# Decoder kernel: the experts' low-rank output in two float32r passes instead of one float32 product

## The chip, the cores and the metric

The kernel runs on one core of a Trainium2 chip. The core has TensorE (PE, matrix products, with a second queue PEld for loading weights), VectorE (DVE), ScalarE (ACT), GpSimd (POOL) and SyncE (SP, which issues most DMAs). Time is device microseconds of the core for one execution; a run takes the kernel before beside a changed one on the same chip.

## The reference, cut to what matters

Two decoder layers over T = 1024 rows of D = 512. The part at hand is the feed-forward of layer 0: a dense product, plus a low-rank output whose rank (8, 16, 32 or 64) is chosen for each row by the largest of four gate scores.

```python
RANKS = (8, 16, 32, 64)
out = jnp.einsum('bsd,od->bso', hidden_states, W) + b
x = hidden_states.reshape(-1, d_in)
scores = x @ gate_w.T + gate_b
...
lora_outputs = jnp.stack([x @ A[:r, :].T @ B[:, :r].T for r in RANKS], axis=1)
sel = jnp.take_along_axis(lora_outputs, selected[:, :, None], axis=1)
...
x = _layernorm(x + _L0_ffn_ref(x, ...), axis=-1)
```

With one expert chosen its weight is 1, so the kernel computes x·Aᵀ (64 columns), sets the columns over the chosen rank to zero, and multiplies by B once. All is float32.

## The kernel before

All engines run programs written out by hand, in order, with semaphores between them. Rows are cut into NT = 8 blocks b of 128. The steps of the feed-forward of layer 0, by engine (line numbers are those of the profile):

- PE `ranks(b)` (L872): x·[Aᵀ, gate columns], 112 columns, into half of a PSUM bank. `ffn_W(b)` (L882): the dense product, four float32 products of 512 columns, into one of three banks (FF_BANK); block b takes the bank of block b-3, so from b = 3 on it waits (L880) for the addition that empties it, `plus` of block b-3. `lora_T(b)` (L886): transposes the masked 64 columns. `lora_out(b)` (L890): adds one float32 product of 65 rows (64 ranks and a row of ones for the bias b) to the bank of `ffn_W(b)`.
- DVE `choose(b)` (L1960 to L1965): four short linked instructions, gate scores, two maxima, mask, and the masked copy `lm`. `ln_head(16+b)`: `plus` (L1804) reads the bank, adds the residual into `rbuf`; then the row statistics (L1788, L1789). `x_low` (L1810): the low part of the normalised, transposed rows.
- ACT `lora_T_out(b)` (L1450): copies the transposed 64 x 128 part into `lmT`. `norm_tail` (L1281) normalises, `x_T_out` (L1274) copies transposed blocks.
- POOL: the reciprocal root of each block's variance.

Between these stand pieces of other work: `early_bends` on ACT (L1224 to L1240) and `unit_part` on DVE (L1739, L1745, L1757) unpack the 4-bit weights of layer 1; `attention_lora`/`add_lora` (L901, L1974) and `attention_product`/`m_low_of` (L912, L1998) fold that layer's attention weights into one matrix; `stack_low_of`, `down_stack_low` (L1980, L1982, L1987) make low parts of small matrices.

The loop over t = 0 to 7 has, on PE, in this order: `lora_T(t)`, two products of `attention_lora` (t up to 3), `ffn_W(t+2)`, `ranks(t+2)`, `lora_out(t)`, and from t = 2 on `x_T(2, t-2)`; from t = 3 on `attention_product` stands among them. `ffn_W(3)`, of t = 1, is the first that waits for a `plus`. On DVE: from t = 3 `x_low`, two `add_lora` (t up to 3), a piece of a low part, unpacking, `choose(t+2)`, `m_low_of`, `ln_head(16+t)`, unpacking. Before the loop DVE does `choose(0)`, `turn_norm(15)`, `choose(1)`; ACT's last step before the loop is `x_T_out(15)`.

A float32r product takes operands rounded to float32r. Elsewhere the kernel already replaces a float32 product by three such passes: high·high, high·low and low·high (L1030 to L1032).

Of the kernel before, what the change touches and what calls it, by code (L numbers as in the profile page):

```python
# [135 lines left out]
def decoder_kernel(nc, i, out):  # L136
# [4 lines left out]
    with ctx:  # L141
        def sb(name, shape, dt=F32):
            return ctx.enter_context(nc.sbuf_tensor(name, shape, dt))
# [24 lines left out]
        with nc.sbuf_tensor("a_down", [STACK, FF], F32) as a_down:  # L168
            pass
        ad_st = sb("ad_st", [STACK, FF], F32R)  # L170
        folded_m = sb("folded", [P, T])
        ff_s = sb("ff_s", [P, SLOTS, 2])
        with nc.sbuf_tensor("arena_r", [P, NF * T], F32R) as arena_r:
# [12 lines left out]
        minus_half = sb("minus_half", [P, 1])  # L186
        small = sb("small", [P, 2, 32])
        gate_v = sb("gate_v", [P, 2, NL + 3 * SEG])
        lmT = sb("lmT", [P, 2, P])
        probT = lmT  # L190
        prob = sb("prob", [P, 2, P])
        threes = prob[:, 0, :]
        qk_b = sb("qk_b", [P, 1])
# [11 lines left out]
        def carve(memory, start, n):  # L205
            return memory[:, start:start + n], start + n
# [21 lines left out]
        qkT, w_at = carve(early_w, w_at, KD * 2 * HA)  # L228
        wv, w_at = carve(early_w, w_at, KD * HA)
        s_qkv, w_at = carve(early_w, w_at, 3 * KD * NB)  # L230
        lm, w_at = carve(early_w, w_at, 2 * RMAX)
        assert w_at <= 2 * CH
        qkT, wv, lm = qkT.rearrange("p (j c) -> p j c", j=KD), wv.rearrange("p (j c) -> p j c", j=KD), lm.rearrange("p (s c) -> p s c", s=2)
        wsum, woT, shared, xT, agT = (m.rearrange("p (j c) -> p j c", j=KD) for m in (wsum, woT, shared, xT, agT))
        w0T = wq1 = shared
        wk1 = [m[:, 0:D] for m in (bT0, bT_d, wk2, wk3)]
        lora_l = wo0
        ad_high = wh[:, :, :].rearrange("p s c -> p (s c)")[:, 0:FF]
        m_lo = [arena_r[:, m_at:m_at + D] for m_at in (wk3_at, free_at, free_at + D, wo0_at)]

# [201 lines left out]
        def _(sp):  # L442
# [159 lines left out]
        def _(pe):  # L602
# [259 lines left out]
            def ranks(b):  # L862
                pe.wait_ge(xt_ready, NT + b + 1)
                if b == 0:
                    pe.wait_ge(in_ffn0, 48)
                    pe.wait_ge(kq_ready, NT - 1)
                elif b == 1:
                    pe.wait_ge(kq_ready, NT)
                if b >= 2:
                    pe.wait_ge(lmT_ready, b - 1)  # L870
                for k in range(KD):
                    last = pe.matmul(turn_bank(b)[:, 0:RMAX + NL], xT[:, k, b * P:(b + 1) * P], agT[:, k, :],  # L872
                                     start=(k == 0), stop=(k == KD - 1))
                last.then_inc(ag_ps, 1)
# [8 lines left out]

            def lora_T(b):
                pe.wait_ge(lm_ready, b + 1)
                pe.transpose(turn_bank(b)[0:RMAX, P:2 * P], lm[:, b % 2, :], ident[:, :]).then_inc(lm_ps, 1)  # L886

            def lora_out(b):
                pe.wait_ge(lmT_ready, b + 1)
                pe.matmul(bank[FF_BANK[b % 3]][:, :], lmT[0:RMAX + 1, b % 2, :], bT0[0:RMAX + 1, :], start=False, stop=True).then_inc(f0_ps, 1)  # L890

            def attention_lora(n):

# [324 lines left out]
        def _(act):  # L1218
# [226 lines left out]
            def lora_T_out(b):  # L1445

                act.wait_ge(lm_ps, b + 1)
                if b >= 2:
                    act.wait_ge(f0_ps, b - 1)
                nc.scalar.activation(lmT[0:RMAX, b % 2, :], turn_bank(b)[0:RMAX, P:2 * P], ACT.Copy).then_inc(lmT_ready, 1)  # L1450

            for t in range(NT):
                lora_T_out(t)
# [270 lines left out]
        def _(dve):  # L1724
# [93 lines left out]
            link(nc.vector.tensor_reduce(k_one[:, 0:1], ident[:, :].rearrange("p (i r) -> p r i", r=ROWG)[:, HD, :], AX.X, ALU.add))  # L1818
            nc.vector.tensor_scalar(k_one[:, 1:2], k_one[:, 0:1], -1.0, None, ALU.mult).then_inc(blanked, 1)
            nc.vector.memset(ones8[:, :, :], 0.0)  # L1820
            nc.vector.memset(lmT[RMAX:RMAX + 1, :, :], 1.0)
            nc.vector.memset(wb[:, 2 * KD:2 * KD + 1], 0.0)
            nc.vector.memset(ones[:, :], 1.0)
            link(nc.vector.memset(picked[:, :], 0.0))
# [128 lines left out]
            def choose(b):  # L1953
                s = b % 2
                ps = turn_bank(b)
                logits, sides, mask = (gate_v[:, s, n:n + size] for n, size in ((0, NL), (NL, 2 * SEG), (NL + 2 * SEG, SEG)))
                dve.wait_ge(ag_ps, b + 1)
                if b == 0:
                    dve.wait_ge(in_bias, 16 * 3)
                link(nc.vector.tensor_tensor(logits, ps[:, RMAX:RMAX + NL], g_b[:, :], ALU.add))  # L1960
                link(nc.vector.tensor_reduce(sides, logits.rearrange("p (n r) -> p n r", r=3), AX.X, ALU.max))
                link(nc.vector.tensor_tensor(mask, sides[:, 0:SEG], sides[:, SEG:2 * SEG], ALU.is_gt))
                if b >= 2:
                    dve.wait_ge(lm_ps, b - 1)
                nc.vector.tensor_tensor(lm[:, s, :].rearrange("p (r m) -> p r m", m=SEG), ps[:, 0:RMAX].rearrange("p (r m) -> p r m", m=SEG),  # L1965
                                        mask.unsqueeze(1).to_broadcast([P, RMAX // SEG, SEG]), ALU.mult).then_inc(lm_ready, 1)

            def add_lora(n):

# [5 lines left out]

            def stack_low_of(part):

                dve.wait_ge(stack_hi, part + 1)
                if part == 0:
                    nc.vector.tensor_tensor(a_st[2 * RG:STACK, :], a_gu[2 * RG:STACK, :], f32(a_st[2 * RG:STACK, :]), ALU.subtract).then_inc(stack_low, 1)  # L1980
                else:
                    nc.vector.tensor_tensor(bd_st[RG:2 * RG, :], bT_d[RG:2 * RG, :], f32(bd_st[RG:2 * RG, :]), ALU.subtract).then_inc(stack_low, 1)  # L1982

            def down_stack_low():

                dve.wait_ge(stack_hi, 4)
                nc.vector.tensor_tensor(ad_st[2 * RG:STACK, :], a_down[2 * RG:STACK, :], f32(ad_high[2 * RG:STACK, :]), ALU.subtract).then_inc(stack_low, 1)  # L1987

            def b_lower(j):

                dve.wait_ge(stack_hi, 4 + j + 1)
                part = b_st[RG:2 * RG, j % 2, :]
                nc.vector.tensor_tensor(part, b_gu[RG:2 * RG, j % 2, :], f32(part), ALU.subtract).then_inc(stack_low, 1)

# [259 lines left out]
def layout(a):  # L2254
# [42 lines left out]
    def pairs(m):  # L2297
# [4 lines left out]
        "qkT": rows(c(qkv[:2 * HA].T)), "wv": rows(c(qkv[2 * HA:].T)), "qk_b": c(f["L0_attn_Wqk_b"].reshape(HA, 2).T.reshape(P, 1)),  # L2302
        "v_b": c(np.concatenate([f["L0_attn_Wv_b"]] * 2)[:, None]), "wo0": wo0,
        "w0T": rows(c(f["L0_ffn_W"].T)), "agT": rows(np.concatenate([f["L0_ffn_A"][rank_at].T, np.stack([gate_w[n] for n in LOGITS], 1)], 1)),
        "bT0": np.concatenate([f["L0_ffn_B"].T[rank_at], f["L0_ffn_b"][None]]), "g_b": np.array([[gate_b[n] for n in LOGITS]], np.float32),
        "c_qkv": pairs(ca[:3].reshape(3 * KD, P, D)), "c_o": pairs(ca[3].T.reshape(KD, P, D)),
        "s_qkv": c(sa[:3].reshape(3, KD, P, NB).transpose(2, 0, 1, 3).reshape(P, -1)),
        "s_o": pairs(sa[3].T.reshape(KD, 2, D)), "lora_l": lora_l, "lora_r": lora_r,
# [25 lines left out]
```

## Time and profile before

| | us |
|---|---|
| median of 3 runs | 645.32 (645.03 to 645.48) |
| the profiled execution | 645.23 |
| its span, first to last instruction | 643.1 |
| PE busy | 632.0 |
| DVE busy | 396.3 |
| ACT busy | 381.6 |

The span is what the trace covers; 2.1 us of the profiled execution lie around it. "Busy" of PE counts from the start of a product to its modelled end, and products overlap, so the distance from one start to the next tells more than the duration. A float32 product appears as two records, a float32r product and a transpose as one.

### The profile page before, as it was taken

The page shows a single profiled execution, that of the slowest core. Times are in us where ns is not written, and L with a number is a line of the kernel's source. Part 1 is how long each engine was busy: PE and PEld are TensorE (multiplying, and loading weights), DVE is VectorE, ACT ScalarE, POOL GpSimd, SP SyncE. Part 2 cuts the span into 40 slices and gives each one's busy share as a digit, 9 for nine tenths or more (in the row PEclk, how much of TensorE's full clock was granted, in tenths as well). Part 3 has the DMA queues.
Part 4 walks back from the last instruction along what each step waited for, and adds up shares of the span by engine and source line. Part 5 has one row for each costly group of instructions (what it writes and reads, how often), then busy time and mean ns, then how long its engine had stood idle before and what let it go on. Part 6 is the DMA issues. An engine that isn't in the chain of part 4 may idle for free.

```text
span 643.1 us, 8521 instructions
## 1 busy us (share of the span) xinstructions
PE 632.0 (98%) x3226; PEld 470.0 (73%) x3226; DVE 396.3 (62%) x633; ACT 381.6 (59%) x527; POOL 65.0 (10%) x116
## 2 busy tenths in 40 slices
PE   9999999999999999999999999999999999999996
PEld 6655555544558888888888888887777888888874
DVE  4798787667988777767667355335655212125467
ACT  2977789976987697576675154223565343316532
POOL 1032142311330000000000000001211000000012
PEclk9999999999999999999999999999999999999999
DMA  7771585512253134233320003056010322100002
GB/s 246 288 243 52 188 268 172 162 52 92 81 152 120 39 110 139 73 104 111 94 83 2 1 1 131 1 216 274 1 33 2 115 77 88 33 1 0 1 33 99
DMA packets 25590, 63.92 MB, mean 99 GB/s; under 512 B 5541, under 2 KB 10725, under 8 KB 24782
## 3 DMA queue, kind: packets, MB, share of 16 engines
q1 hardware_dynamic: 23294, 61.68, 29.4%
q10 hardware_dynamic: 2256, 1.70, 0.8%
q8 instruction: 26, 0.43, 0.3%
q14 instruction: 14, 0.11, 0.1%
HBM read 58.77 MB, written 4.60 MB: 99 GB/s over the span
## 4 chain that ended last, share of the span: by engine, by line
PE 88%; DVE 4%; ACT 4%; DMA 1%; issue 1%; SPq 1%; POOL 0%; POOLq 0%; DVEq 0%; ACTq 0%
PE bank L1043 18%; PE bank L1031 8%; PE bank L1030 8%; PE bank L1032 8%; PE bank L1122 8%; PE bank L1121 8%; PE bank L882 4%; PE bank L802 3%; PE bank L606 3%; PE bank L741 2%; PE bank L1097 1%; DMA codes<-in_c_qkv 1%; PE bank L912 1%; PE bank L926 1%; PE bank L984 1%
## 5 line engine op out<-in xcount | busy, mean ns | idle before, releaser
L1232 ACT ACTIVATE line<-line 128x1024 f32<-128x1024 f32 x87 | 91.4, 1050 | 0.2
L1030 PE MATMUL bank<-xh,wh 128*128 128x512 f32 x224 | 87.5, 391 | 0.0
L1031 PE MATMUL bank<-xl,wh 128*128 128x512 f32 x224 | 87.5, 391 | 0.0
L1032 PE MATMUL bank<-xh,wl 128*128 128x512 f32 x224 | 87.3, 390 | 0.0
L1043 PE MATMUL bank<-wh,xh 128*128 128x512 f32 x192 | 76.1, 396 | 0.2 <-DVE xl L2128 0.2
L1043 PE MATMUL bank<-wh,xl 128*128 128x512 f32 x192 | 74.9, 390 | 0.0
L2211 DVE SCALAR_TENSOR_TENSOR arena<-bank,ff_s,arena 128x512 f32<-128x512 f32 x28 | 21.0, 752 | 72.9 <-PE bank L1122 63.8
L2128 DVE TENSOR_TENSOR xl<-arena,xh 128x1024 fp32r<-128x1024 f32 (+1 forms) x26 | 29.7, 1141 | 35.4 <-ACT xh L1536 35.3
L1121 PE MATMUL bank<-xh,wh 128*128 128x512 f32 x128 | 50.3, 393 | 0.0
L1536 ACT ACTIVATE xh<-arena 128x1024 fp32r<-128x1024 f32 (+1 forms) x26 | 25.6, 991 | 41.3 <-PE bank L1043 34.8
L1122 PE MATMUL bank<-xl,wh 128*128 128x512 f32 x128 | 49.9, 390 | 0.0
L1032 PEld LDWEIGHTS bank<-xh,wl 128*128 128x128 f32 x224 | 42.1, 188 | 8.8
L1030 PEld LDWEIGHTS bank<-xh,wh 128*128 128x128 f32 x224 | 42.1, 188 | 8.5
L1031 PEld LDWEIGHTS bank<-xl,wh 128*128 128x128 f32 x224 | 42.1, 188 | 8.5
L1630 ACT ACTIVATE arena<-bank,ff_s 128x512 f32<-128x512 f32 x28 | 19.2, 686 | 43.4 <-PE bank L1122 43.4
L1512 ACT ACTIVATE arena<-bank 128x512 f32<-128x512 f32 x28 | 16.4, 586 | 46.9 <-PE bank L1032 46.9
L1695 POOL TENSOR_TENSOR rstd<-rstd,minus_half 128x1 f32<-128x1 f32 x40 | 26.7, 668 | 172.1 <-DVE rstd L2149 162.4
L1043 PEld LDWEIGHTS bank<-wh,xh 128*128 128x128 f32 x192 | 36.1, 188 | 8.3 <-DVE xl L2128 0.6
L1043 PEld LDWEIGHTS bank<-wh,xl 128*128 128x128 f32 x192 | 36.1, 188 | 7.5
L1121 PE MATMUL bank<-xh,wl 128*128 128x512 f32 x96 | 37.6, 391 | 0.0
L1745 DVE SCALAR_TENSOR_TENSOR line<-line 128x1024 f32<-128x1024 f32 x29 | 35.3, 1218 | 3.6 <-ACT line L1232 3.2
L1043 PE MATMUL bank<-wl,xh 128*128 128x512 f32 x96 | 37.4, 390 | 0.0
(219 smaller groups left out, 1264.3 us busy)
## 6 DMA issues: line engine op xcount, KB each, us to landing
codes<-in_c_gu SPq DMA_DIRECT2D x14, 512.0 KB, 3.8
scales<-in_s_gu SPq DMA_DIRECT2D x28, 256.0 KB, 4.0
codes<-in_t_gu SPq DMA_DIRECT2D x8, 512.0 KB, 4.2
codes<-in_c_dn SPq DMA_DIRECT2D x7, 512.0 KB, 4.6
scales<-in_s_dn SPq DMA_DIRECT2D x14, 256.0 KB, 3.9
fold<-in_t_dn SPq DMA_DIRECT2D x1, 3584.0 KB, 15.7
codes<-in_c_qkv SPq DMA_DIRECT2D x6, 512.0 KB, 4.8
scales<-in_t_gu SPq DMA_DIRECT2D x6, 512.0 KB, 3.8
```

Of the source, the lines that this page charges most:

```text
L882: pe.matmul(bank[FF_BANK[b % 3]][:, :], xT[:, k, b * P:(b + 1) * P], w0T[:, k, :], start=(k == 0), stop=False)
L1030: pe.matmul(dst, wh[:, s, c:c + P], xh[:, k, cols], start=(k == 0), stop=False)
L1031: pe.matmul(dst, wh[:, s, c:c + P], xl[:, k, cols], start=False, stop=False)
L1032: last = pe.matmul(dst, wl[:, s, c:c + P], xh[:, k, cols], start=False, stop=(k == KD - 1))
L1043: ins = pe.matmul(dst, h[:, b * P:(b + 1) * P], w, start=first and p == 0, stop=last and p == len(hiddens) - 1)
L1121: pe.matmul(dst, w[:, c:c + P], xh[:, k, cols], start=(k == 0), stop=False)
L1122: last = pe.matmul(dst, w[:, c:c + P], xl[:, k, cols], start=False, stop=(k == KD - 1))
L1232: nc.scalar.activation(below(slot), below(slot), ACT.Prelu, bias=bias, scale=scale, alpha=alpha).then_inc(bent, 1)
L1536: nc.scalar.activation(dst[:, cols], hT[:, j, cols], ACT.Copy).then_inc(done, 1)
L1695: last = nc.gpsimd.tensor_tensor(rstd[:, m % 2, 1:2], rstd[:, m % 2, 0:1], minus_half[:, :], ALU.pow)
L1745: nc.vector.scalar_tensor_tensor(weight(slot), weight(slot), -NEAR_UP, below(slot), ALU.max, ALU.subtract).then_inc(joined, 1)
L2128: nc.vector.tensor_tensor(low[:, cols], hT[:, j, cols], f32(hi[:, cols]), ALU.subtract).then_inc(done, 1)
```

## The change

The 64 masked columns are split into a high part (rounded to float32r) and a low part (the rest), 64 columns each, side by side; they are transposed as one 128 x 128 block [low; high]. Then the product is made in two float32r passes that add to the same bank:

- first pass, `lm_both` (128 rows: low, high) times `b_both` (128 rows: high of B, low of B): low·high + high·low;
- second pass, `lm_one` (97 rows: high; the rest are ones) times `b_high_one` (high of B; bias high; 31 rows of zeros; bias low).

What is added on the engines: on DVE in each `choose` a copy (rounding) and a subtraction, each linked to the one before; once `experts_low`, two subtractions, between `turn_norm(15)` and `choose(1)`. On ACT a second copy in each `lora_T_out`, and once `experts_high`, four instructions, after `x_T_out(15)` and ahead of `lora_T_out(0)`. `experts_low` waits for `experts_high`, and `experts_high` waits for the loads and for the write-out of `beta_s`, whose memory `lm_one` takes over. The load `bT0` (65 x 512) becomes two, `b_two` (128 x 512) and `b_one` (97 x 512). A memset of DVE's start goes.

```diff
             def lora_T(b):
                 pe.wait_ge(lm_ready, b + 1)
-                pe.transpose(turn_bank(b)[0:RMAX, P:2 * P], lm[:, b % 2, :], ident[:, :]).then_inc(lm_ps, 1)
+                pe.transpose(turn_bank(b)[:, P:2 * P], lm[:, b % 2, :], ident[:, :]).then_inc(lm_ps, 1)
 
             def lora_out(b):
                 pe.wait_ge(lmT_ready, b + 1)
-                pe.matmul(bank[FF_BANK[b % 3]][:, :], lmT[0:RMAX + 1, b % 2, :], bT0[0:RMAX + 1, :], start=False, stop=True).then_inc(f0_ps, 1)
+                if b == 0:
+                    pe.wait_ge(lm_ready, 2)
+                pe.matmul(bank[FF_BANK[b % 3]][:, :], lm_both[:, b % 2, :], b_both, start=False, stop=False)
+                pe.matmul(bank[FF_BANK[b % 3]][:, :], lm_one[0:ONE_ROWS.stop, b % 2, :], b_high_one[0:ONE_ROWS.stop, :], start=False, stop=True).then_inc(f0_ps, 1)
...
-                nc.scalar.activation(lmT[0:RMAX, b % 2, :], turn_bank(b)[0:RMAX, P:2 * P], ACT.Copy).then_inc(lmT_ready, 1)
+                nc.scalar.activation(lm_both[:, b % 2, :], turn_bank(b)[:, P:2 * P], ACT.Copy)
+                nc.scalar.activation(lm_one[0:RMAX, b % 2, :], turn_bank(b)[RMAX:P, P:2 * P], ACT.Copy).then_inc(lmT_ready, 1)
+
+            def experts_high():
+
+                act.wait_ge(in_ffn0, 64)
+                act.wait_ge(kb_out, 16 * KD)
+                for n in range(2):
+                    nc.scalar.activation(lm_one[ONE_ROWS, n, :], ident[ONE_ROWS, :], ACT.Identity, bias=1.0, scale=0.0)
+                nc.scalar.activation(b_both, b_two, ACT.Copy)
+                nc.scalar.activation(b_high_one[0:ONE_ROWS.stop, :], b_one[0:ONE_ROWS.stop, :], ACT.Copy).then_inc(stack_hi, 1)
+
+            experts_high()
...
-            nc.vector.memset(lmT[RMAX:RMAX + 1, :, :], 1.0)
...
-                nc.vector.tensor_tensor(lm[:, s, :].rearrange("p (r m) -> p r m", m=SEG), ps[:, 0:RMAX].rearrange("p (r m) -> p r m", m=SEG),
-                                        mask.unsqueeze(1).to_broadcast([P, RMAX // SEG, SEG]), ALU.mult).then_inc(lm_ready, 1)
+                chosen, high = lm[:, s, 0:RMAX], lm_high[:, s, RMAX:P]
+                link(nc.vector.tensor_tensor(chosen.rearrange("p (r m) -> p r m", m=SEG), ps[:, 0:RMAX].rearrange("p (r m) -> p r m", m=SEG),
+                                             mask.unsqueeze(1).to_broadcast([P, RMAX // SEG, SEG]), ALU.mult))
+                link(nc.vector.tensor_copy(high, chosen))
+                nc.vector.tensor_tensor(chosen, chosen, f32(high), ALU.subtract).then_inc(lm_ready, 1)
+
+            def experts_low():
+
+                dve.wait_ge(stack_hi, 1)
+                low, row = slice(RMAX, P), slice(RMAX + ROWG, RMAX + ROWG + 1)
+                nc.vector.tensor_tensor(b_both[low, :], b_two[low, :], f32(b_both[low, :]), ALU.subtract)
+                nc.vector.tensor_tensor(b_high_one[row, :], b_one[row, :], f32(b_high_one[row, :]), ALU.subtract)
...
             choose(0)
             turn_norm(2 * NT - 1)
+            experts_low()
             choose(1)
             dve.wait_ge(kq_ps, NT)
```

DVE, from `choose(0)` to the plus of block 0: before, `choose(1)` (L1960 to L1965) follows `turn_norm(15)` (L1800).

```order
L1800 TENSOR_SCALAR x<-rbuf,mv,rstd 128x512
L1960 TENSOR_TENSOR gate_v<-bank,g_b 128x48
L1961 TENSOR_REDUCE gate_v<-gate_v 128x16
L1962 TENSOR_TENSOR gate_v<-gate_v 128x8
L1965 TENSOR_TENSOR early_w<-bank,gate_v 128x64
L1974 TENSOR_TENSOR arena<-arena,bank 128x512 x2
L1739 SCALAR_TENSOR_TENSOR line<-line 128x1024
L1745 SCALAR_TENSOR_TENSOR line<-line 128x1024
```

The same place now; the new rows are L2000 and L2001 (`experts_low`), L1993 and L1994.

```order
L1826 TENSOR_SCALAR x<-rbuf,mv,rstd 128x512
L2000 TENSOR_TENSOR arena_r<-arena,arena_r 64x512
L2001 TENSOR_TENSOR arena_r<-arena,arena_r 1x512
L1985 TENSOR_TENSOR gate_v<-bank,g_b 128x48
L1986 TENSOR_REDUCE gate_v<-gate_v 128x16
L1987 TENSOR_TENSOR gate_v<-gate_v 128x8
L1991 TENSOR_TENSOR early_w<-bank,gate_v 128x64
L1993 CAST wl<-early_w 128x64
L1994 TENSOR_TENSOR early_w<-early_w,wl 128x64
L2009 TENSOR_TENSOR arena<-arena,bank 128x512 x2
```

Four instructions stand between `turn_norm(15)` and the first `add_lora` that did not stand there, and the first of them waits for ACT.

ACT, from the last transposed block of layer 0's second norm on, before:

```order
L1274 ACTIVATE arena<-bank 128x4x128
L1450 ACTIVATE lmT<-bank 64x128
L1224 ACTIVATE line<-codes 128x1024
L1226 ACTIVATE line<-codes 128x1024
L1232 ACTIVATE line<-line 128x1024
```

And now:

```order
L1288 ACTIVATE arena<-bank 128x4x128
L1472 ACTIVATE lm_one<-ident 33x128 x2
L1473 ACTIVATE arena_r<-arena 128x512
L1474 ACTIVATE arena_r<-arena 97x512
L1464 ACTIVATE lm_both<-bank 128x128
L1465 ACTIVATE lm_one<-bank 64x128
L1238 ACTIVATE line<-codes 128x1024
```

`experts_high` (L1472 to L1474) stands behind the copy of the last block (L1288), although its inputs were loaded long before.

PE, from `ranks(2)` to `ffn_W(3)`, before and now: the order stays, one product (L890) becomes two (L903, L904).

```order
L872 MATMUL bank<-arena 128x112 x4
L890 MATMUL bank<-arena,lmT 128x512
L886 MATMUL bank<-ident,early_w 64x128
L901 MATMUL bank<-early_w,arena 128x512 x2
L882 MATMUL bank<-arena 128x512 x4
```

```order
L883 MATMUL bank<-arena 128x112 x4
L903 MATMUL bank<-arena_r,lm_both 128x512
L904 MATMUL bank<-arena_r,lm_one 128x512
L897 MATMUL bank<-ident,early_w 128x128
L915 MATMUL bank<-early_w,arena 128x512 x2
L893 MATMUL bank<-arena 128x512 x4
```

Here only the pair L903, L904 is new, and the transpose L897 is 128 instead of 64 wide.

## Rows read from the trace of the kernel before

**Rows 1.** The page, busy us, share of the span and instructions by engine.

```profile
PE 632.0 (98%) x3226; PEld 470.0 (73%) x3226; DVE 396.3 (62%) x633; ACT 381.6 (59%) x527; POOL 65.0 (10%) x116
```

**Rows 2.** Busy time by stretch: us; busy of each engine (count); clock; DMA; GB/s.

```profile
137.00:157.00 20.00, 20.00 (x70) 9.50 (x70) 18.90 (x36) 15.04 (x20) 4.95 (x9) 1.00 0.35 105
```

**Rows 3.** The chain that ended last, in order of time: start us, us, what.

```profile
137.31 0.87 PE bank L890 x2
...
139.36 3.63 PE bank L882 x8
...
186.95 0.23 PE bank L927
```

**Rows 4.** Timeline of PE: start us, us, line, tiles, shape, idle before and its releaser.

```profile
145.84 3.70 PE L882 MATMUL bank<-arena 128*128 128x512 f32 x8
...
152.83 3.70 PE L882 MATMUL bank<-arena 128*128 128x512 f32 x8
...
182.54 0.63 PE L606 MATMUL bank<-ident,x 128*128 128x128 f32 x4 [0.19 <-DVE xl L1810]
```

**Rows 5.** Timeline of ACT, around the two places that price its new instructions.

```profile
132.17 0.26 ACT L1450 ACTIVATE lmT<-bank 64x128 f32<-64x128 f32 x1
132.32 1.05 ACT L1224 ACTIVATE line<-codes 128x1024 f32<-128x1024 int32 x1
...
138.15 0.62 ACT L1408 ACTIVATE a_st<-early_w 96x512 fp32r<-96x512 f32 x1
138.67 0.25 ACT L1450 ACTIVATE lmT<-bank 64x128 f32<-64x128 f32 x1
```

**Rows 6.** Timeline of DVE, from choose(1) to the plus of block 2.

```profile
127.79 0.21 DVE L1960 TENSOR_TENSOR gate_v<-bank,g_b 128x48 f32<-128x48 f32 x1 [2.52 <-PE bank L872]
...
128.47 0.22 DVE L1965 TENSOR_TENSOR early_w<-bank,gate_v 128x64 f32<-128x64 f32 x1
132.89 1.28 DVE L1974 TENSOR_TENSOR arena<-arena,bank 128x512 f32<-128x512 f32 x2 [4.20 <-PE bank L901]
...
137.35 0.21 DVE L1960 TENSOR_TENSOR gate_v<-bank,g_b 128x48 f32<-128x48 f32 x1 [0.71 <-PE bank L872]
...
138.22 0.69 DVE L1804 TENSOR_TENSOR rbuf<-x,bank 128x512 f32<-128x512 f32 x1
...
144.88 0.68 DVE L1804 TENSOR_TENSOR rbuf<-x,bank 128x512 f32<-128x512 f32 x1
...
151.52 0.68 DVE L1804 TENSOR_TENSOR rbuf<-x,bank 128x512 f32<-128x512 f32 x1
```

**Rows 7.** DVE's one copy from SBUF to SBUF: duration ns min/median/max.

```profile
L1817 DVE COPY fold<-ident x1: 227/227/227, 4.6 to 4.6; 128x128 f32<-128x128 f32 x1
```

**Rows 8.** Timeline of DVE: a subtraction on partitions 64 to 95, and what follows it.

```profile
142.20 0.68 DVE L1980 TENSOR_TENSOR a_st<-early_w,a_st 32x512 fp32r<-32x512 f32 x1
142.92 1.23 DVE L1739 SCALAR_TENSOR_TENSOR line<-line 128x1024 f32<-128x1024 f32 x1
```

**Rows 9.** Timeline of DVE, choose(5), choose(6), and the x_low that PE waits for.

```profile
161.10 0.21 DVE L1960 TENSOR_TENSOR gate_v<-bank,g_b 128x48 f32<-128x48 f32 x1 [3.73 <-PE bank L872]
...
168.37 2.02 DVE L1987 TENSOR_TENSOR ad_st<-a_down,wh 32x1792 fp32r<-32x1792 f32 x1
170.49 0.21 DVE L1960 TENSOR_TENSOR gate_v<-bank,g_b 128x48 f32<-128x48 f32 x1
...
181.71 0.68 DVE L1810 TENSOR_TENSOR xl<-bank,xh 128x512 fp32r<-128x512 f32 x1
```

**Rows 10.** Timeline of PE: two groups of one shape at the start, the last product.

```profile
1.08 3.78 PE L614 MATMUL bank<-fold 128*128 128x256 f32 x8 [1.08 <-POOL fold L1683]
...
7.31 1.03 PE L614 MATMUL bank<-fold 128*128 128x256 f32 x4
...
636.57 0.39 PE L1043 MATMUL bank<-wh,xl 128*128 128x512 f32 x1
```

**Rows 11.** Busy time by stretch, as rows 2, after the last product.

```profile
640.00:641.00 1.00, 0.00 (x0) 0.00 (x0) 0.74 (x2) 0.00 (x0) 0.17 (x1) 0.72 0.23 84
```

More of the change, by code:

```diff
@@ L170, in decoder_kernel @@
         ad_st = sb("ad_st", [STACK, FF], F32R)
+        with nc.sbuf_tensor("lm_one", [P, T], F32R) as lm_one:
+            pass
         folded_m = sb("folded", [P, T])
@@ L188, in decoder_kernel @@
         gate_v = sb("gate_v", [P, 2, NL + 3 * SEG])
-        lmT = sb("lmT", [P, 2, P])
-        probT = lmT
+        with nc.sbuf_tensor("lm_both", [P, 2, P], F32R) as lm_both:
+            pass
+        probT = sb("probT", [P, 2, P])
         prob = sb("prob", [P, 2, P])
@@ L217, in decoder_kernel @@
         agT, at = carve(arena, at, KD * (RMAX + NL))
+        b_low_at = at
         bT0, at = carve(arena, at, D)
@@ L221, in decoder_kernel @@
         bT_d, at = carve(arena, at, D)
+        b_high_at = at
         wk2, at = carve(arena, at, D)
@@ L230, in decoder_kernel @@
         s_qkv, w_at = carve(early_w, w_at, 3 * KD * NB)
-        lm, w_at = carve(early_w, w_at, 2 * RMAX)
-        assert w_at <= 2 * CH
+        lm = early_w[:, FF:2 * CH]
+        assert w_at <= 2 * CH and 2 * CH - FF == 4 * RMAX and 2 * RMAX == P
+        lm_high = wl[:, :, :].rearrange("p s c -> p (s c)")[:, FF:2 * CH].rearrange("p (s c) -> p s c", s=2)
         qkT, wv, lm = qkT.rearrange("p (j c) -> p j c", j=KD), wv.rearrange("p (j c) -> p j c", j=KD), lm.rearrange("p (s c) -> p s c", s=2)
@@ L237, in decoder_kernel @@
         lora_l = wo0
+        b_two, b_one = wk3, m_free[:, 0:D]
+        b_both, b_high_one = arena_r[:, b_low_at:b_low_at + D], arena_r[:, b_high_at:b_high_at + D]
+        ONE_ROWS = slice(RMAX, RMAX + ROWG + 1)
+        lm_one = lm_one[:, 0:2 * P].rearrange("p (s t) -> p s t", s=2)
         ad_high = wh[:, :, :].rearrange("p s c -> p (s c)")[:, 0:FF]
@@ L535, in _ @@
             sp.dma_start(w0T, i["w0T"]).then_inc(in_ffn0, 16)
-            sp.dma_start(bT0[0:RMAX + 1, :], i["bT0"]).then_inc(in_ffn0, 16)
+            sp.dma_start(b_two, i["b_two"]).then_inc(in_ffn0, 16)
+            sp.dma_start(b_one[0:ONE_ROWS.stop, :], i["b_one"]).then_inc(in_ffn0, 16)
             load_scales(C_O)
@@ L864, in ranks @@
                 if b == 0:
-                    pe.wait_ge(in_ffn0, 48)
+                    pe.wait_ge(in_ffn0, 64)
                     pe.wait_ge(kq_ready, NT - 1)
@@ L1976, in stack_low_of @@
             def stack_low_of(part):
-                dve.wait_ge(stack_hi, part + 1)
+                dve.wait_ge(stack_hi, 1 + part + 1)
                 if part == 0:
@@ L1984, in down_stack_low @@
             def down_stack_low():
-                dve.wait_ge(stack_hi, 4)
+                dve.wait_ge(stack_hi, 1 + 4)
                 nc.vector.tensor_tensor(ad_st[2 * RG:STACK, :], a_down[2 * RG:STACK, :], f32(ad_high[2 * RG:STACK, :]), ALU.subtract).then_inc(stack_low, 1)
             def b_lower(j):
-                dve.wait_ge(stack_hi, 4 + j + 1)
+                dve.wait_ge(stack_hi, 1 + 4 + j + 1)
                 part = b_st[RG:2 * RG, j % 2, :]
@@ L2304, in layout @@
         "w0T": rows(c(f["L0_ffn_W"].T)), "agT": rows(np.concatenate([f["L0_ffn_A"][rank_at].T, np.stack([gate_w[n] for n in LOGITS], 1)], 1)),
-        "bT0": np.concatenate([f["L0_ffn_B"].T[rank_at], f["L0_ffn_b"][None]]), "g_b": np.array([[gate_b[n] for n in LOGITS]], np.float32),
+        "b_two": np.concatenate([f["L0_ffn_B"].T[rank_at]] * 2),
+        "b_one": np.concatenate([f["L0_ffn_B"].T[rank_at], f["L0_ffn_b"][None], np.zeros((ROWG - 1, D), np.float32), f["L0_ffn_b"][None]]), "g_b": np.array([[gate_b[n] for n in LOGITS]], np.float32),
         "c_qkv": pairs(ca[:3].reshape(3 * KD, P, D)), "c_o": pairs(ca[3].T.reshape(KD, P, D)),
```

## The prediction, made blind

> **What bounds the kernel now.** I read the page's busy times first: PE is busy 632.0 of 643.1 us [rows 1], so a gain on PE counts only where nothing else stands between, and a PE that waits costs at full price. The change lies between 121 and 195 us, so the second view is the busy time by stretch there: from 137 to 157 us PE is busy 20.00 of 20 us, but DVE 18.90 [rows 2]. Two engines are full at once. The third view is DVE's timeline [rows 6]: it waits 0.71 us ahead of choose(2) at 137.35 and then not again until it waits 3.73 us at 161.10 [rows 9]. The fourth is where PE depends on DVE. From ffn_W(3) on PE needs the bank that DVE's plus of three blocks earlier empties. That plus starts at 138.22 and ends at 138.91; ffn_W(3) starts on PE at 139.29 (139.36 in the chain, which counts from the end of the work before it) [rows 6, 3]. The margin is 0.4 us. Late in the loop DVE is already ahead on the chain: PE waits 0.19 us at 182.54 for x_low [rows 4].
>
> **PE's gain.** The float32 product of lora_out takes 0.87 us of the chain, a float32r product of 512 columns 0.23 [rows 3]. Two take 0.46 to 0.47, so each of the 8 blocks saves 0.40 us, 3.2 us in all. The wider transpose costs nothing: a transpose takes its columns from the moving side, 128 before and now. Its weights and the new ones load behind running products, as now. This 3.2 us is an upper bound of the gain.
>
> **experts_high on ACT.** It stands where lora_T_out(0) started, at 132.17 [rows 5]. An instruction of 64x128 there gives way to the next after 0.15 us, one of 96x512 after 0.52 and ends after 0.62 [rows 5]. Two tiny ones, the first large one and the last: 132.17 + 0.30 + 0.52 + 0.62 = 133.61. The loads were issued some 50 us before, and the extra 190 KB queue behind no one who is near the path. ACT's own delay of 1.5 us is hidden: it waits for others again before it is waited for.
>
> **experts_low on DVE** starts 0.04 us later, at 133.65, although DVE has been idle since turn_norm(15), which ends before 127.79 [rows 6]. Its two subtractions touch few partitions but 512 columns, which takes 0.68, and the one of this kind that is there lets its follower start after 0.72 [rows 8]. So it ends its hold at 135.09. That is 0.12 us more each than the 0.60 at which whole-tile subtractions follow each other. The Trainium skill (VectorE: DVE Perf Modes, section on two Vector instructions with no wait between them) says that an instruction whose operands start in another quadrant of partitions is held until all earlier ones have finished; rows 8 agree, and by overlap instead the sum below would be 0.24 us less.
>
> **choose grows.** Of choose(1), 0.68 us pass before its fourth instruction [rows 6]. That one now has to end before the copy: 0.22 + 0.04. The copy of 64 columns lies between the 0.17 us of an 8-column instruction of choose and the 0.227 of a 128-column copy [rows 7]: 0.19 + 0.04. The subtraction gives way after 0.15, as the fourth instruction did. Each choose grows by 0.26 + 0.23 = 0.49 us (bounds 0.3, if the copy is much cheaper, and 0.6).
> By the Trainium skill (same page, the perf-mode tier table) a float32 copy within SBUF runs at twice the rate of a two-input operation; for 64 columns that would take some 0.03 us off each choose, 0.2 us off the sum, and the single row here is of another shape.
>
> **The sum, along the path.** Shifts against the trace of before:
> - choose(1) now runs from 135.09 and takes 0.68 + 0.49 + 0.15 = 1.32, so add_lora starts at 136.41 instead of 132.89: +3.52. The idle 0.71 ahead of choose(2) takes part of it: +2.81. choose(2) adds 0.49: the plus of block 0 starts at +3.30, 141.52, and ends at 142.20.
> - PE, 0.40 early, stands at ffn_W(3) at 138.96 and starts 0.15 after the plus ends (the distance between x_low's end, 182.39, and PE at 182.54 [rows 9, 4]): 142.35, +3.06. PE idles 3.4 us. This is the price of where experts_low stands.
> - DVE has no idle for two more rounds and gains 0.49 in each. Plus of block 1 starts at 144.88 + 3.79, so ffn_W(4) at 149.50: +3.66 (PE was there at 148.50). Plus of block 2 at 151.52 + 4.28, ffn_W(5) at 156.63 instead of 152.83: +3.80.
> - At 161.10 DVE waits for PE again, so it follows PE: +3.80. choose(5) makes +4.29. Ahead of choose(6) DVE had 0.1 us to spare [rows 9]: +4.2, then +4.7, and choose(7) +5.2. So x_low ends at 187.6 and PE's transposes stand at +5.2 instead of 182.54.
> - lora_out(7) comes after that and still saves 0.40: **+4.8 us** at the end of the loop. From there both queues move as a whole: PE waits once more for ACT by 0.3 us and then fills the rest, so nothing is made up.
> The profiled execution took 645.23, 0.09 under the median, which I let stand: 645.2 + 4.8 = **650.0**. Its own range: 648.0 (growth of choose 0.3, some 1.2 us less in six rounds, and the hold of experts_low 0.3 shorter, with 0.5 of spare time unseen in the waits) to 651.0 (growth 0.6, waits of PE 0.1 longer).
>
> **Rivals.**
> - *PE alone sets the pace* (5 in 100), the faster side. If DVE takes its additions in its idle time, as its 62% of the span suggests, all eight savings count: 645.2 - 3.2 = 642.0. Against it stand DVE's 18.90 busy of 20 us in the very stretch, and the margin of 0.4 us at ffn_W(3). It decides as long as the plus of block 0 is late by under 0.4 us.
> - *The gains and the losses cancel* (5 in 100): the wait at ffn_W(3) costs 3.06, but choose's two new steps are hidden behind waits that the timeline doesn't show, and the later savings count. Then DVE is at +2.81 from block 0 on, ffn_W(3) at +2.6, and with the savings of lora_out(3) to (7) 2.0 less: +0.6, 645.8.
> - *Only the first wait counts in full* (12 in 100): as the last, with DVE still on the path at 182.54: +2.6 to there, less 0.40: +2.2 to 2.5, 647.6.
> - *PE's clock falls in the wait* (18 in 100). Now PE has no wait this long. At the end of the program it does: its last product ends at 636.96, and in the stretch from 640 to 641 the mean granted clock is 0.72 [rows 10, 11], so from about 640.44 on it is at 1.2 GHz instead of 2.4, 3.5 us after PE stopped. The new idle is 3.4 us. What the low level costs is bounded by the start, where eight records of L614 take 3.78 us and later four of the same shape 1.03 [rows 10]: 3.8 us of work at half rate lose 1.9 us. Some 0.5 of them hide behind DVE at choose(3): +1.4, 651.4; were it to last twice as long, 653.
>  The Trainium skill (TensorE: Matmul & The Clock Gate, section on the HAM clock gate) says that the half rate is the default and that an idle PE returns to it; rows 11 agree for the program's end, and no row here shows it for a wait within the program.
> - *The new path isn't ready* (2 in 100): experts_high also waits for the write-out of beta_s. SP issues it at 125.26 to 126.4, 5.8 us before ACT is there, and the pieces are small. Late by 2 us it would give 652.
>
> **How the numbers follow.** The forecast itself, DVE's new steps on the path with the clock kept, has 58 in 100; with the others that is 58 + 5 + 5 + 12 + 18 + 2 = 100. A measurement of this kernel can tell about 0.2%, 1.3 us, from no change. Slower by more than that: the forecast, the first wait alone, the clock, the late write-out: 90. Within: 5. Faster: 5. The range of 8 in 10 takes in the forecast, the clock at 651.4 and the first-wait case: 647.3 to 652.0; outside it lie the first two rivals and the tails of the others.
>
> **What would show each step.** In the profile after: the pair of float32r products at 0.23 each; ACT's four new instructions from 132.2 on, without a wait; DVE's idle ahead of experts_low until 133.65 and its two at 0.72 distance; one wait of PE of 3.4 us before ffn_W(3) for DVE's plus, then about 1.0 and 0.5 before ffn_W(4) and (5); and PE's transposes at 187.7. The prediction is wrong if PE doesn't wait at ffn_W(3), or if DVE catches up between 139 and 161 us, which asks for steps of choose under 0.2 us together. Granted clock under 1.00 after 142 us would tell the fourth rival.

## The result, and the profile after

The changed kernel takes **655.35 us** (median of 4 runs, 654.58 to 657.0), the kernel before 645.4 beside it: ratio 1.0158, interval 1.0146 to 1.017. It is slower, as forecast, but by 10.0 us where 4.8 were forecast, and outside the range. The profiled execution took 657.0 us (span 655.1, before 643.1), the slowest of the four, so its trace shows up to 1.6 us more than the median has.

The page, busy time by engine, as [rows 1]:

```profile
PE 632.8 (97%) x3226; PEld 471.0 (72%) x3226; DVE 400.6 (61%) x650; ACT 386.1 (59%) x539; POOL 64.8 (10%) x116
```

PE's busy time did not fall by 3.2 us, it rose by 0.8; part of it ran at the lower clock. In the stretch of [rows 2] PE now works 16.19 of 20 us, and two stretches of 8 us show the clock. Busy time by stretch, kernel after:

```profile
137.00:157.00 20.00, 16.19 (x53) 7.62 (x53) 15.76 (x36) 16.12 (x25) 1.95 (x3) 0.91 0.18 53
...
144.00:152.00 8.00, 4.76 (x11) 1.90 (x8) 7.59 (x16) 5.61 (x9) 1.95 (x3) 0.81 0.11 36
104.00:112.00 8.00, 5.23 (x11) 2.44 (x12) 6.85 (x12) 7.97 (x13) 2.02 (x3) 0.79 0.18 66
```

The last of these lies before anything that the prediction spoke of. First ACT's timeline, the same step in the kernel before and then after (in brackets the idle time ahead, and its releaser):

```profile
96.47 0.69 ACT L1373 ACTIVATE heads<-bank,wb 128x512 f32<-128x512 f32 x1 [0.98 <-PE bank L802]
```

```profile
102.09 0.69 ACT L1387 ACTIVATE heads<-bank,wb 128x512 f32<-128x512 f32 x1 [6.49 <-DMA kq<-heads]
```

PE's timeline, kernel after:

```profile
104.96 0.66 PE L617 MATMUL bank<-ident,x 128*128 128x128 f32 x4 [1.91 <-ACT x L1295]
107.43 1.58 PE L795 MATMUL bank<-heads,prob 128*128 128x512 f32 x2 [1.82 <-DVE prob L1914]
...
142.36 0.48 PE L903 MATMUL bank<-arena_r,lm_both 128*128 128x512 f32 x1
142.68 0.40 PE L904 MATMUL bank<-arena_r,lm_one 97*128 97x512 f32 x1
142.91 0.27 PE L897 MATMUL bank<-ident,early_w 128*128 128x128 f32 x1
...
147.68 5.40 PE L893 MATMUL bank<-arena 128*128 128x512 f32 x8 [3.24 <-DVE rbuf L1830]
...
192.27 0.50 PE L903 MATMUL bank<-arena_r,lm_both 128*128 128x512 f32 x1 [1.22 <-ACT lm_one L1465]
...
194.29 0.63 PE L617 MATMUL bank<-ident,x 128*128 128x128 f32 x4 [1.28 <-DVE xl L1836]
...
205.42 0.63 PE L617 MATMUL bank<-ident,x 128*128 128x128 f32 x4 [0.47 <-DVE xl L1836]
```

Three things are to be seen. ACT waits 6.49 us for a write-out of kq that it didn't wait for before, and PE loses two waits of 1.9 and 1.8 us by it. The forecast wait before ffn_W(3) is there, 3.24 us at 147.68, and the group behind it takes 5.40 us instead of 3.70. And PE waits again at 192, 194 and 205 us. All in all everything is 5.3 us late by the last x_T before the first low-rank product (136.32, before 131.04), and 12.0 us late where the gate and up products of layer 1 start (L1044; 228.25, before 216.26); nothing more is lost behind it.

DVE, kernel after, with the steps that the prediction costed:

```profile
139.27 0.69 DVE L2000 TENSOR_TENSOR arena_r<-arena,arena_r 64x512 fp32r<-64x512 f32 x1 [8.24 <-ACT arena_r L1474]
139.97 0.69 DVE L2001 TENSOR_TENSOR arena_r<-arena,arena_r 1x512 fp32r<-1x512 f32 x1
140.68 0.21 DVE L1985 TENSOR_TENSOR gate_v<-bank,g_b 128x48 f32<-128x48 f32 x1
...
141.35 0.22 DVE L1991 TENSOR_TENSOR early_w<-bank,gate_v 128x64 f32<-128x64 f32 x1
141.61 0.20 DVE L1993 CAST wl<-early_w 128x64 fp32r<-128x64 f32 x1
141.84 0.23 DVE L1994 TENSOR_TENSOR early_w<-early_w,wl 128x64 f32<-128x64 f32 x1
141.99 1.27 DVE L2009 TENSOR_TENSOR arena<-arena,bank 128x512 f32<-128x512 f32 x2
```

### The profile page after: what moved, and what is told of

It is laid out like the page before. It is cut to its first block, busy times and chain, and to the rows that moved or that the text cites. A ratio compares the mean times of both kernels' runs of the same rounds, so it can differ in the third digit from the quotient of the medians.

```text
span 655.1 us, 8553 instructions
## 1 busy us (share of the span) xinstructions
PE 632.8 (97%) x3226; PEld 471.0 (72%) x3226; DVE 400.6 (61%) x650; ACT 386.1 (59%) x539; POOL 64.8 (10%) x116
## 4 chain that ended last, share of the span: by engine, by line
PE 79%; DVE 9%; DMA 4%; ACT 3%; issue 2%; POOL 1%; SPq 1%; POOLq 0%; DVEq 0%; ACTq 0%
PE bank L1057 18%; PE bank L1045 8%; PE bank L1044 8%; PE bank L1046 8%; PE bank L1136 8%; PE bank L1135 8%; PE bank L617 3%; PE bank L893 2%; PE bank L813 2%; DMA kq<-heads 2%; PE bank L752 2%; DMA codes<-in_c_qkv 1%; PE bank L1111 1%; DVE line L1771 1%; PE bank L998 1%
## 5 line engine op out<-in xcount | busy, mean ns | idle before, releaser
L1044 PE MATMUL bank<-xh,wh 128*128 128x512 f32 x224 | 87.5, 390 | 0.0
L1044 PEld LDWEIGHTS bank<-xh,wh 128*128 128x128 f32 x224 | 42.1, 188 | 8.5
L1136 PE MATMUL bank<-xl,wl 128*128 128x512 f32 x96 | 37.4, 390 | 0.0
```

The costliest lines, as they stand in the source:

```text
L1044: pe.matmul(dst, wh[:, s, c:c + P], xh[:, k, cols], start=(k == 0), stop=False)
L1136: last = pe.matmul(dst, w[:, c:c + P], xl[:, k, cols], start=False, stop=(k == KD - 1))
```

## The experiments

The times beside each are medians; "before" is the kernel before, measured beside them (645.3 to 645.6 us).

### 1. The load of 97 rows

Bytes or rows? The change adds 320 KB to the loads (b_two 256, b_one 194, the old bT 130 gone). But b_one has 97 rows, and 97 is prime. The kernel before was given one more load at that place, of 97 or 96 rows, into columns of m_free that nobody reads; nothing else was changed but the count that PE waits for.

```
+            sp.dma_start(m_free[0:97, 0:D], i["more"]).then_inc(in_ffn0, 16)
...
-                    pe.wait_ge(in_ffn0, 48)
+                    pe.wait_ge(in_ffn0, 64)
```

> The kernel before with one load more, 97 x 512 float32 (194 KB) into memory that nothing reads, issued where the change issues its second new load, and waited for with the others by ranks(0). Nothing is computed with it. Theory A, the load's row count: 97 divides by none of 2 to 16, so all its rows lie on one of the 16 DMA engines, which is busy with them for some 10 us; the sixteenth part of every later transfer lands late, the write-out of kq that keys_column_out(3) waits for among them. Then ACT waits 5 to 7 us at 95.5 and the run is 4 to 6 us slower than before. Rival B, the extra bytes or ScalarE's other waits of the changed kernel: 194 KB at some 300 GB/s are under 1 us of all engines, so the run stays within 0.5 us of before.

> The same with 96 rows, that is 1% fewer bytes and a number that 16 divides. Theory A (row count): six rows lie on each engine, and the time is that of before within 0.5 us, with no wait of ACT for the write-out of kq. Rival B (bytes): the same as with 97 rows.

With 97 rows: 648.32 us, 1.0044 [1.0028, 1.006]. With 96: 645.11, 0.9991 [0.9982, 1.0001]. One row more costs 3.2 us. ACT with 97 rows, then the page's rows on DMA issues for 78 to 104 us (KB each, median us to landing) of the kernels with 97 and with 96 rows:

```profile
100.71 0.69 ACT L1374 ACTIVATE heads<-bank,wb 128x512 f32<-128x512 f32 x1 [4.79 <-DMA kq<-heads]
```

```profile
kq<-heads SPq DMA_DIRECT2D x4, 256.0 KB, 9.4
...
codes<-in_c_o SPq DMA_DIRECT2D x1, 512.0 KB, 13.0
```

```profile
kq<-heads SPq DMA_DIRECT2D x4, 256.0 KB, 5.4
...
codes<-in_c_o SPq DMA_DIRECT2D x1, 512.0 KB, 5.5
```

The increments of the semaphores in the trace say how. In the kernel after, the load of b_one is issued at 81.1 and the last increment of in_ffn0 comes at 99.54 us. The write-out of kq issued at 88.06 has 15 of its 16 increments by 92.15, the last at 102.00; in before all 16 lie between 91.69 and 92.18. The other transfers of that time show the same picture, 15 parts in time and one late: by 7 to 10 us for those issued up to 91 us, by 4 to 6 for the next ones. So one of the 16 DMA engines carries all 194 KB, and a 16th of every later transfer queues behind it. The Trainium skill (DMA: Bandwidth & Descriptors, section "Why a DMA increments its semaphore by 16 and not by 1") gives the rule: a transfer is spread over the largest number up to 16 that divides its slowest dimension; 65 rows, as before, go to 13 engines, 96 or 128 to 16, and 97 to one. The runs agree, for 96, 97 and 128.

The same on the changed kernel: b_one gets 31 rows of zeros and is loaded as 128.

```
-            sp.dma_start(b_one[0:ONE_ROWS.stop, :], i["b_one"]).then_inc(in_ffn0, 16)
+            sp.dma_start(b_one[:, :], i["b_one"]).then_inc(in_ffn0, 16)
```

> The changed kernel with b_one padded by zeros to 128 rows and loaded whole; the products still read 97 rows. Theory A: the wait for the write-out of kq (6.5 us on ACT, 3.7 us on PE, and 3.4 us of half clock) goes, all up to 130 us stands as before, and the run falls from +10.0 to about +4.8 us against before if the clock holds in the remaining wait of PE at ffn_W(3), to about +6.2 if it falls there too. Rival B: no change, still +10 us.

652.06 us, 1.0102 [1.0087, 1.0117]: the rows cost 3.3 us of the 10 (3.5 if each kernel is taken against the kernel before that was measured beside it). The kq wait is gone. PE from 137 us, and the clock (PE busy, clock, DMA share, GB/s):

```profile
142.25 5.08 PE L893 MATMUL bank<-arena 128*128 128x512 f32 x8 [3.24 <-DVE rbuf L1830]
...
186.52 0.50 PE L903 MATMUL bank<-arena_r,lm_both 128*128 128x512 f32 x1 [1.22 <-ACT lm_one L1465]
...
188.54 0.63 PE L617 MATMUL bank<-ident,x 128*128 128x128 f32 x4 [1.29 <-DVE xl L1836]
...
189.11 5.30 PE L893 MATMUL bank<-arena 128*128 128x512 f32 x8
```

```profile
138.00:146.00 8.00, 4.76 (x10) 0.79 0.02 10
186.00:194.00 8.00, 6.19 (x16) 0.79 0.53 147
```

This is the kernel that the prediction described, without the missed load: 6.5 us over the 645.58 measured beside it, where 4.8 was forecast, and 6.2 if the clock fell.

### 2. The first wait

The same kernel, with experts_high one block earlier in ScalarE's queue and experts_low behind choose(1) instead of ahead of it; a semaphore of its own tells PE that the split is done.

```
+                if t == NT + 1:
+                    experts_high()
...
-            experts_high()
...
-                    pe.wait_ge(lm_ready, 2)
+                    pe.wait_ge(experts_split, 1)
...
+            choose(1)
             experts_low()
-            choose(1)
             dve.wait_ge(kq_ps, NT)
```

> As the one before, and the split of B is moved: experts_high ahead of ACT's last x_T_out of layer 0's second norm (a gap of 3.2 us in the trace of before), experts_low behind choose(1), and lora_out(0) waits for a semaphore of its own. Theory C (the held DVE queue is the cause of PE's wait at ffn_W(3), and each choose costs 0.49 us of DVE's time on the path): PE waits 0.3 us there instead of 3.2, the clock stays at 2.4 GHz, and what is left are the additions of choose in rounds 1, 2, 5, 6 and 7, less PE's savings: +2.0 us against before. Rival D (the additions of choose are nearly free, only the hold counts): -2 us or better.

648.44 us, 1.0045 [1.003, 1.006]: the wait at ffn_W(3) shrinks from 3.24 to 0.44 us, and 3.6 us come back. Of these 2.8 are the wait. For the clock the profiled executions are no fair sample. In the one of this kernel it doesn't fall (mean granted clock 0.999, 647.74 us), but the other three have 0.994 (648.24 to 648.88 us). A mean of 0.994 is some 7.8 us at 1.2 GHz by my estimate (0.006 times 2 times the span), where 0.999 to 0.996, as in the kernel before, is 1 to 5 us; so at least one fall lies within the program in each of the three, and no trace shows where. With 128 rows alone the mean is 0.992 in the profiled execution and 0.996 in the others. So the 3.6 us are the wait and what it did; that the clock was saved is not shown. What is left of the slowdown is 2.9 us, with PE's gain in it.

### 3. choose's two steps

The kernel of 2 without the copy and the subtraction in choose; it leaves the low part of the masked columns out of the result.

```
-                link(nc.vector.tensor_copy(high, chosen))
-                nc.vector.tensor_tensor(chosen, chosen, f32(high), ALU.subtract).then_inc(lm_ready, 1)
```

> The kernel after with b_one loaded as 128 rows and the split of the second stack before experts_high (as in after_128_rows_early_split, 648.44 us), and without the two DVE steps that choose gained (the copy of the chosen columns and the subtraction); the other 64 columns of lm are zeros, so the low part of the low-rank activations is left out of the computation. It asks what is left of the slowdown once the first wait and the wide load are gone. Theory D (the rest comes from DVE's longer choose, 0.36 us in each of eight blocks, that makes x_T and x_low late for TensorE): the waits of TensorE of 0.4 to 1.3 us between 150 and 200 us mostly go and TensorE's gain shows, 3.2 us under 645.3 at best, so 642 to 644 us. Theory E (ScalarE's queue is what is late: its second copy of 0.27 us in each block, and the copies of 1.04 us that stand ahead of it): the wait of 1.21 us at lora_out stays, and the time is 646 to 648 us.

645.19 us, 0.9997 [0.9987, 1.0007]. The two steps cost 3.25 us. Some of it may come by the clock: here 7 of 10 executions have a mean of 0.999, of kernel 2 one of four. That one took 647.74 us, the seven 645.15 in the middle: 2.6 us. DVE has no gap in this stretch, so their 0.49 us come back in every round. DVE's plus in three blocks in a row, first with the steps (kernel of 2), then without:

```profile
139.00 0.68 DVE L1830 TENSOR_TENSOR rbuf<-x,bank 128x512 f32<-128x512 f32 x1
...
146.13 0.68 DVE L1830 TENSOR_TENSOR rbuf<-x,bank 128x512 f32<-128x512 f32 x1
...
153.27 0.68 DVE L1830 TENSOR_TENSOR rbuf<-x,bank 128x512 f32<-128x512 f32 x1
```

```profile
138.40 0.68 DVE L1830 TENSOR_TENSOR rbuf<-x,bank 128x512 f32<-128x512 f32 x1
...
145.04 0.68 DVE L1830 TENSOR_TENSOR rbuf<-x,bank 128x512 f32<-128x512 f32 x1
...
151.69 0.68 DVE L1830 TENSOR_TENSOR rbuf<-x,bank 128x512 f32<-128x512 f32 x1
```

7.13 us a round with the steps, 6.64 and 6.65 without, 6.66 and 6.64 before [rows 6]. PE's round was 6.55 and 6.99 [rows 4]; it would now be 0.39 less: ffn_W(2) to (3) takes 6.17 here, before 6.56. So even with the steps gone PE's gain doesn't show: two rounds stay at DVE's 6.65 us, at 181 us PE waits 1.28 us for ScalarE, and right behind that 0.37, and at 193 us 0.46, for DVE's x_low. The time lies between those of the two theories on record, D below 644 and E above 646.

### 4. Can the gain be collected?

The low part of the down stack was moved: 2.02 us of DVE ahead of choose(6) (the first expectation calls it 3.7; the traces have 2.02 [rows 9]). First to the top of the round before, in both kernels.

```
+                if t == 3:
+                    down_stack_low()
...
-                if t == 4:
-                    down_stack_low()
```

> As after_128_rows_early_split (648.44 us), and also with the low part of the down stack (3.7 us of VectorE) put ahead of x_low of the block before the one it stood in, where VectorE was idle. If the waits of TensorE between 175 and 195 us come from VectorE's queue behind those 3.7 us, they shrink by 1 to 2.5 us in sum and the time is 646.0 to 647.5 us; if they come from ScalarE's queue, the time stays within 0.7 us of 648.4; if the moved step now delays x_T or x_low of its own block, TensorE waits there up to 3 us and the time is 649 to 651 us.

> The kernel before with that one move alone. TensorE waited for nothing of VectorE's there over 0.2 us, so the time is 645.0 to 645.6 us, no change, if VectorE has room for the step in the earlier block; up to 3 us more (648 us) if it has not.

648.32 us, 1.0045 [1.0028, 1.0063], no gain; and 647.09, 1.0029 [1.0018, 1.004], slower by 1.8. There it stands ahead of that round's x_low and additions (add_lora). In the kernel before DVE first waits 0.97 us for ScalarE's part of it, and PE then waits for the additions; in the changed kernel a new wait of 1.21 us stands at the same place. PE in the kernel before with the move:

```profile
159.13 3.70 PE L912 MATMUL bank<-arena 128*128 128x512 f32 x8 [1.57 <-DVE arena L1974]
```

For before the second case on record came true: that PE "waited for nothing of VectorE's there" says nothing of the room in DVE's queue.

Then into the gap itself, directly ahead of choose(5):

```
-                if t == 4:
+                if t == 3:
                     down_stack_low()
                 if t + 2 < NT:
                     choose(t + 2)
```

> The kernel after with b_one loaded as 128 rows and the early split (648.44 us), and with the low part of the down stack (2.02 us of VectorE) put in the gap of 3.15 us in which VectorE waits for choose(5), and not, as in the move that won nothing, ahead of add_lora of that block. If VectorE's queue ahead of block 6 is what makes ScalarE's lm_one and x_low late for TensorE there (waits of 1.21 and 1.28 us), both shrink to under 0.3 us and the time is 646.0 to 646.9 us. If ScalarE's own copies are late, the wait of 1.21 us stays and the time is 647.5 to 648.5 us.

647.29 us, 1.003 [1.0018, 1.0042]: 1.2 us less than kernel 2, with intervals that overlap. The wait for lm_one stays (1.28, in kernel 2 1.21); x_low's went from 1.28 to 0.80. In between the two theories. Next the two other stacks' subtractions (0.68 us each) left DVE's full rounds too, for its idle time behind block 6:

```
-                if t in (1, 2):
-                    stack_low_of(t - 1)
...
+                if t == 6:
+                    stack_low_of(0)
+                    stack_low_of(1)
```

> As that, and also with the two subtractions of 0.68 us of the other stacks taken out of blocks 1 and 2, where VectorE is busy without a gap, and put behind block 6, where it idles 1.6 us. VectorE's share of those blocks falls from 7.14 to 6.46 us, under TensorE's 6.6. Theory F (TensorE's gain is there, but blocks 1 to 7 go at VectorE's pace, so the gain shows as soon as VectorE is made shorter): the waits of 0.44, 0.91 and 0.48 us go too, and the time is 642.5 to 645.0 us, a little under the kernel before. If something else holds the blocks to 7.1 us, the time is 646 to 648 us.

> The kernel before with the same three moves. There TensorE sets the pace and waits for nothing of VectorE's over 0.2 us, so by theory F the moves win nothing: 644.9 to 645.5 us. If they win here what they win in the other kernel, the gain was never the changed product's: 641 to 643 us.

646.46 us, 1.0016 [1.0008, 1.0025], and 645.12, 0.9995 [0.9986, 1.0003]. The waits in the full rounds, those before ffn_W(3), (4) and (5), fell from 0.43, 0.91 and 0.47 to 0.43 and 0.43, so DVE did hold them; the time is above theory F's 645.0, because the pair of waits at 181 us stays, with a fall of the clock behind it in the profiled execution. That fall comes and goes: the four executions with a mean clock of 0.994 or 0.995 took 647.0 to 647.4 us, the four with 0.998 or 0.999 645.3 to 646.5. The first wait of the pair is for ScalarE, which runs without a gap from 169 to 182 us and has lm_one behind 2.1 us of unpacking. The second, for x_low, ends last, and DVE has no gap before it from 172 us on. ScalarE, DVE, then PE:

```profile
177.54 2.14 ACT L1246 ACTIVATE line<-line 128x1024 f32<-128x1024 f32 x2
179.59 0.58 ACT L1288 ACTIVATE xh<-bank 128x512 fp32r<-128x512 f32 x1
180.06 0.27 ACT L1475 ACTIVATE lm_both<-bank 128x128 fp32r<-128x128 f32 x1
180.34 0.27 ACT L1476 ACTIVATE lm_one<-bank 64x128 fp32r<-64x128 f32 x1
```

```profile
180.26 1.21 DVE L1783 SCALAR_TENSOR_TENSOR fold<-line,scales 128x1024 f32<-128x1024 f32 x1
181.38 0.68 DVE L1836 TENSOR_TENSOR xl<-bank,xh 128x512 fp32r<-128x512 f32 x1
```

```profile
180.67 0.50 PE L903 MATMUL bank<-arena_r,lm_both 128*128 128x512 f32 x1 [1.27 <-ACT lm_one L1476]
...
182.21 1.08 PE L617 MATMUL bank<-ident,x 128*128 128x128 f32 x4 [0.80 <-DVE xl L1836]
```

Before, the answering copy ran at 180.28 and PE came for it at 181.33: ScalarE had 0.8 us to spare, less than PE now gains by that block. So the last pair puts those three copies ahead of the unpacking, and x_low ahead of one step of DVE's:

```
+                if t == 5:
+                    x_T_out(2 * NT + t - 2, dst=xh)
+                    lora_T_out(6)
                 for u, h in half_plan(3, t, 1):
                     unit_bends(u, h)
```

> The kernel after_128_rows_vector_relieved (646.46 us) with one more change, in ScalarE's and VectorE's queues of block 5: xh of block 3 and the two copies of the low-rank rows of block 6 go ahead of the two copies of 1.04 us of the unpacking, and x_low of block 3 ahead of one step of 1.21 us. If those 2.1 us of unpacking are what makes lm_one late for the product of block 6 (waits 1.27 and 0.80 us, and the clock's fall behind them), both waits go, the clock does not fall, and the time is 643.3 to 644.6 us, under the kernel before. If the unpacking moved behind them then makes x of the next block late, TensorE waits for that instead and the time stays 645.5 to 646.5 us.

> The kernel before with all the same moves. TensorE had no wait of over 0.2 us there, so nothing to win: 644.9 to 645.4 us. If they win here too, the gain of the other kernel isn't the changed product's.

645.79 us, 1.001 [1.0001, 1.0019], above the 643.3 to 644.6 of the theory, and 645.07, 0.9999 [0.999, 1.0008], as expected. The wait for lm_one is gone, and the one for x_low is longer by the time that PE now comes earlier, with DVE full up to it. PE goes on at 180.97 instead of 182.21: 1.24 us earlier, as x_low, which was moved ahead of a step of 1.21 us. So of the pair DVE's wait set the time, and ScalarE's stood in front of it:

```profile
180.97 0.63 PE L617 MATMUL bank<-ident,x 128*128 128x128 f32 x4 [1.20 <-DVE xl L1840]
...
193.16 0.63 PE L617 MATMUL bank<-ident,x 128*128 128x128 f32 x4 [0.98 <-DVE xl L1840]
```

No version beat the kernel before. With all these repairs the change is still worth nothing (0.7 us slower than the kernel before with the same moves): what PE saves it waits for, in the end for DVE alone.

## Why the prediction was wrong, by its steps

- **The failed step** is "The loads were issued some 50 us before, and the extra 190 KB queue behind no one who is near the path". The extra is 320 KB, but that is not the fault. The step asked when the loads are needed and not what they delay: kq's write-out, issued on the same engines 7 us later, is near the path. The load costs 3.3 to 3.5 us of the 10.0 (experiment 1), and 2.7 in the kernel before. Counting bytes would not have found it; 96 rows cost nothing.
- **The first wait** was right: 3.24 us against 3.4, and a shift of 3.11 us from the transposes at 136.32 to ffn_W(3) against +3.06. ScalarE's four instructions take from 137.57 to 139.24, 1.67 us against 1.44. DVE's two subtractions give way after 0.70 and 0.71, against 0.72 from [rows 8].
- **choose** grew by 0.26 + 0.23, as forecast. The copy took 0.20, between the bounds from [rows 7], and the two-input operation of 64 columns behind it 0.23. The Trainium skill (VectorE: DVE Perf Modes, the perf-mode tier table) gives a float32 copy twice the rate of such an operation. At 64 columns that would be 0.03 us (an estimate from the page's rate), and the two durations don't speak against it; in the sum it is nothing, since the forecast had taken 0.19 for the copy already.
- **The clock** was the second step to fail: the forecast itself stood on "the clock kept" (58 in 100), and the rival with 18 in 100 came. Behind the 3.24 us wait the trace grants half rate (1.2 GHz) from 148.92 to 152.33, 3.41 us, and the group of 3.70 takes 5.40, here and almost so in the kernel with 128 rows (5.08). Without the 5.28 us of before 137 us, ffn_W(4) and (5) start at +4.92 and +5.07 against +3.66 and +3.80: 1.27 us net, against the rival's 1.9 less 0.5. The weak part was the chance: the wait was called as long as what precedes the fall at the program's end [rows 11], and that should have made this the likeliest case, 651.4.
- **The late rounds** were right in what they add up to. Counted in the same way, choose(5), (6) and (7) start at +5.07, +5.48 and +5.97, and PE's transposes at +6.47: the forecast's 3.80, 4.2, 4.7 and 5.2, each with the clock's 1.27. What the prediction never read is ScalarE, whose spare 0.8 us were less than PE gains by then: it makes the wait of 1.22 at 192 us. That wait didn't set the time, since the one for x_low stands behind it.
- **The last saving** was to count ("still saves 0.40"). It doesn't: PE comes early and waits 0.47 us at 205.42 for x_low, where it had no wait before, and the shift goes from +6.47 to +6.7 and not to +6.1.
- So the profiled execution adds up: 5.3 (load) + 4.8 (forecast) + 1.3 (clock) + 0.6 (last saving and wait) = 12.0. It lies 1.6 us above the median; how much of each part the median has, its trace can't say. By the medians of the runs the way down from the changed kernel is load 3.3, first wait 3.6, choose's steps 3.25, together 10.15. This is no check of the sum, since each kernel holds the change of the one before; it ends 0.1 to 0.2 us under the kernel before. "An upper bound of the gain", 3.2 us, was right to call it so; nearly none of it was kept.

What stays open: where the clock falls in executions that weren't profiled, and by what share. All four of the changed kernel have a mean of 0.994, like the profiled one with its two falls (at 107.96 and 148.92 us), so the median probably has both. In the kernel before with 97 rows PE's two waits at the first place are 0.21 and 1.81 us, and the clock stayed at 1.00 from 104 to 112 us; so part of the 0.6 to 0.8 us by which the same load costs more in the changed kernel may be the clock. No experiment separates them.

## What to carry to other kernels

Price a new load not only by when it is needed but by what is issued behind it, and look at its row count first: 97 rows, a prime number, went to one DMA engine, and one 16th of every later transfer waited. Where a second engine is as full as the busiest (VectorE's 6.65 us a round beside TensorE's 6.55), a saving on the busiest is worth nothing until the other is made shorter too, and each instruction added to the other is paid in full, round by round. Where PE waits twice in a row, the wait that ends last is the one to mend. Read the spare time of every engine that feeds the bound one, in each round, before counting a gain. And read the mean clock of every execution before calling a profiled one typical.

## What the hardware showed that was not expected

- A 97-row load of 194 KB took from 81.1 to 99.5 us, while the loads of 128x512 land in 5.9 and 6.8 us in the kernel with 128 rows, and it made one part in 16 of the transfers behind it 4 to 10 us late.
- The clock fell behind waits of 1.2 to 1.9 us: two of 1.22 and 1.29 us (which end at 186.52 and 188.54), then half rate from 189.45 to 192.86 in the kernel with 128 rows (clock 0.79 in 186 to 194); two of 1.91 and 1.82 us in the kernel after (0.79 in 104 to 112). It doesn't always: with 1.21 and 1.28 us at the same place it stayed at full rate in the profiled execution of experiment 2, while the three others of that kernel have a mean of 0.994.
- Two float32r products of 512 columns start 0.32 us apart, and the next instruction 0.23 us later (142.36, 142.68, 142.91). From the start of the product before them (ranks) to the transpose behind them it is 1.36 us, with the float32 product it was 1.75 (136.27 to 138.02): 0.39 us saved a block, against 0.40 forecast.
